# Normalising the rows of a second LayerNorm on GpSimd instead of VectorE, with five score products one unit earlier

## The reference

```python
x = x + xattn(layernorm(x), ctx, ctx, mask, Wq, bq, Wk, bk, Wv, bv, Wo, bo, 16)   # 16 heads of 16
x = x + ffn(layernorm(x), Ws1, bs1, Ws2, bs2, We1, be1, We2, be2, Wr, br)

def layernorm(x, eps=1e-5):
    m, v = mean(x, -1), var(x, -1)
    return (x - m) / sqrt(v + eps)
```

## Time and profile before

| | us |
|---|---|
| runs | 1044.37 median of 3 (1043.41 to 1051.45) |
| profiled execution | 1049.24 |
| its span | 1047.6 |
| PE busy in the span | 944.4 (90%) |
| DVE busy | 709.0 (68%) |
| ACT busy | 577.4 (55%) |
| POOL busy | 380.3 (36%) |
| slots begin (first transpose of the maxima, line 537) | 60.8, 99.1, 141.5, 184.5, 227.4, 270.4, 313.0, 357.0 |

### The profile page before, as it was taken

The page is one execution under the profiler, slowest core; times in us unless marked ns, Lnnn a source line. Parts: engine busy times, 40 slices in busy tenths (PEclk is TensorE's granted clock), DMA queues, the critical chain, the costliest instruction groups (busy, mean ns, idle before and its releaser), DMA issues.

```text
span 1047.6 us, 26860 instructions
## 1 busy us (share of the span) xinstructions
PE 944.4 (90%) x7515; PEld 691.6 (66%) x7515; DVE 709.0 (68%) x1822; ACT 577.4 (55%) x1296; POOL 380.3 (36%) x547
## 2 busy tenths in 40 slices
PE   5588999999997887979999799999799999999996
PEld 4223445545453345758778698888588888888885
DVE  5776778888787545636686666777357667667753
ACT  3126566665655564323544565677346666656653
POOL 5300131635526252142420443444323443433342
PEclk9779999999999989989999999999999999999999
DMA  4543424455253131247554553455224544535232
GB/s 153 136 103 75 107 70 120 134 135 135 73 151 94 34 141 61 62 179 240 198 190 128 155 138 54 132 134 142 41 36 129 143 92 96 137 49 141 44 53 43
DMA packets 107927, 117.34 MB, mean 112 GB/s; under 512 B 20396, under 2 KB 99960, under 8 KB 107648
## 3 DMA queue, kind: packets, MB, share of 16 engines
q1 hardware_dynamic: 87168, 67.97, 23.7%
q0 software_dynamic: 20064, 47.20, 18.1%
q10 hardware_dynamic: 560, 0.53, 0.1%
HBM read 73.91 MB, written 38.87 MB: 108 GB/s over the span
## 4 chain that ended last, share of the span: by engine, by line
PE 38%; issue 6%; DMA 5%; DVE 3%; SPq 2%; ACT 1%; ACTq 1%; DVEq 0%; another core or an unknown queue 0%; POOL 0%; POOLq 0%
PE ff_psH L2329 22%; PE ff_psY L2356 13%; DMA ff_xrow<-expert_in 2%; PE ff_psX L2283 2%; DMA ff_x<-out_dram 1%; DVE ff_actf L2582 1%; DMA ff_xrow<-xn 1%; PE ff_psH L2298 1%; DMA expert_in<-ff_zeros 1%; PE ff_psY L2313 1%; DMA out_dram<-ff_x 1%; DVE ff_actl L2575 1%; SPq L1995 0%; ACT ff_gel L2423 0%; DVE ff_ysb L2659 0%
## 5 line engine op out<-in xcount | busy, mean ns | idle before, releaser
L2329 PE MATMUL ff_psH<-xh,ff_wx 128*128 128x256 f16 (+1 forms) x1776 | 269.6, 263 | 15.4 <-issue 10.3
L2329 PE MATMUL ff_psH<-xl,ff_wx 128*128 128x256 f16 (+1 forms) x888 | 217.5, 263 | 0.0
L1136 DVE TENSOR_REDUCE fast_negm<-fast_psS 128x2 f32<-128x512 f32 x256 | 167.8, 686 | 72.9 <-PE fast_psS L515 70.4
L894 ACT ACTIVATE fast_PT<-fast_psT 128x512 f32<-128x512 f32 x256 | 147.0, 595 | 94.2 <-PE fast_psT L547 92.7
L2264 POOL DMA_INDIRECT out_dram<-ff_ysc,ff_trow x78 | 124.8, 1600 | 195.8 <-ACT ff_ysc L2471 181.5
L2329 PEld LDWEIGHTS ff_psH<-xh,ff_wx 128*128 128x128 f16 x1776 | 166.7, 99 | 37.3 <-issue 14.8
L2582 DVE SCALAR_TENSOR_TENSOR ff_actf<-ff_psH,ff_b1T,ff_gel 128x256 f32<-128x256 f32 (+1 forms) x234 | 106.1, 454 | 103.5 <-ACT ff_gel L2423 102.0
L2423 ACT ACTIVATE ff_gel<-ff_psH,ff_b1T 128x256 f32<-128x256 f32 (+1 forms) x234 | 105.4, 451 | 83.2 <-PE ff_psH L2329 64.0
L2356 PE MATMUL ff_psY<-ff_wx,ff_acth 128*128 128x256 f16 x792 | 132.4, 273 | 0.6 <-DVE ff_actl L2575 0.5
L2418 ACT ACTIVATE ff_acth<-ff_actf 128x256 f16<-128x256 f32 (+1 forms) x282 | 110.7, 393 | 34.4 <-DVE ff_actf L2582 32.8
L515 PE MATMUL fast_psS<-fast_Kz,fast_Qs 128*128 128x512 f16 x256 | 101.2, 400 | 24.8 <-DVE fast_negm L1136 16.9
(11 more groups left out here) (279 smaller groups left out, 1691.8 us busy)
## 6 DMA issues: line engine op xcount, KB each, us to landing
ff_st<-in_L_ffn_We_dram POOLq DMA_DIRECT2D x12, 1536.0 KB
ff_xrow<-expert_in SPq DMA_DIRECT2D x41, 256.0 KB
ff_st<-in_L_ffn_We_dram POOLq DMA_DIRECT2D x12, 768.0 KB
fast_Qs<-qstk SPq DMA_DIRECT2D x48, 128.0 KB
fast_xbuf<-in_x_dram SPq DMA_DIRECT2D x8, 512.0 KB, 3.9
fast_words<-in_mask_BxSxS_bk_dram SPq DMA_DIRECT2D x8, 512.0 KB
fast_xres<-in_x_dram SPq DMA_DIRECT2D x8, 512.0 KB, 4.2
out_dram<-fast_x1s SPq DMA_DIRECT2D x8, 512.0 KB, 5.4
```

The source lines that it names most:

```text
L894: nc.scalar.activation(PT[:, n % NPT, :], psT[n % 2][:], ACT.Exp).then_inc(sem["exp_done"], 1)
L1136: nc.vector.tensor_reduce(negm[:, two(b), t, 2 * p:2 * p + 2], src, AX.X, ALU.max, negate=True).then_inc(sem["max_done"], 1)
L2329: mm = nc.tensor.matmul(psH[j % stage.banks][:, (half + 1) * NB - rows:(half + 1) * NB], a[:, dt, lo:lo + P], x[:, dt, NB - rows:], start= ...
```

## The change

The four normalising instructions of the second norm go from VectorE's list to GpSimd's, right behind rstd2 of the same batch; the semaphore xn2_ready, for which TensorE and SP wait, is now raised by GpSimd. In `SCORES` unit 1 gets 5 products instead of 4 and unit 6 gets 4 instead of 5, for TensorE and VectorE alike; the running sums are 5, 10, 15, 19, 24, 28, 32 where they were 4, 9, 14, 18, 23, 28, 32. A place for a maximum in VectorE's unit 1 goes; the maximum itself is taken a line later by `rest`.

```diff
-SCORES = (0, 4, 5, 5, 4, 5, 5, 4)
+SCORES = (0, 5, 5, 5, 4, 5, 4, 4)
...
             begin(1)
             if real(b - 1):
                 normalised_out(b - 1, 1)
-            one_maximum()
-            if real(b - 2):
-                ln2(b - 2)
             rest()
...
             normalised_out(last, 1)
-            ln2(last - 1)
             early_blocks.row_low(dve, 0)
...
             low(1, 0)
-            ln2(last)
             gate(1, 2)
...
+        def ln2(b):
+            until(pool, "rstd2", of("rstd2", b, 1))
+            for t in range(QT):
+                ins = nc.gpsimd.tensor_scalar(xn2_of(b)[:, t, 0:D], xres[:, t, :], mv2[:, t, 0:1], rstd2[:, t:t + 1],
+                                              ALU.subtract, ALU.mult)
+            ins.then_inc(sem["xn2_ready"], 1)
+
...
             if real(b - 2):
                 rstd2_(b - 2)
+                ln2(b - 2)
             if real(b - 4) and not left_over(b - 4):
                 rows_out(b - 4)
```

## The result

The changed kernel takes **1061.9 us** by the median of 4 runs (1058.55 to 1064.15), the kernel before, run beside it, 1044.03 (4 runs, 1043.41 to 1051.45). The ratio on record for the runs side by side is 1.014, 95% interval 1.0116 to 1.0164: slower by some 15 us (12 to 17). The two medians by themselves lie 17.9 us apart; with four runs of each, the four of before spread over 8 us, that is the coarser measure. The forecast was 1047.9 and no change; the range ended at 1056.

A forecast was written before the change was run, and what follows sets the result against it. TensorE's own queue was taken as the bound. Slot 6, slot 7 and tail -0.3, VectorE beside GpSimd +1.5 and +0.6, products +1.7 gave +3.5 us: 1047.9 us, range 1041 to 1056.

The forecast's parts named there:

- part 2: The four normalising instructions on GpSimd: 2.8 us taken, between 0.9 and 3.7; middle slots would not wait for the rows.
- the addition: GpSimd's adding of a vector to the same xres rows, 2.78 us for four, taken as the nearest row for the duration.
- rival B: More contention: at 3.7 us on GpSimd the queue shifts 2.6, x1s also covers the comparison; +7.8 us, 1052.2, chance 0.12.
- 1.7 for the products: Cost of the moved score products on TensorE: +0.34 us in each of slots 1 to 5.
- the forecast's 1.5 for contention: Slots 3 to 5: GpSimd's shifted bias on xres slows VectorE's cast, gap and pick, 0.5 us each slot.
- Part 1: Four instructions leave VectorE: worth nothing to TensorE in slots 2 to 5, up to 1.2 us once in slot 6.
- The 1.2 us wait in slot 6: TensorE's product waiting 1.23 us for a maximum queued behind VectorE's four normalising instructions; the removal was to save it.
- Part 3: GpSimd's queue behind the four comes 1.7 us later, beside VectorE's work: 1.5 us in slots 3 to 5, 0.6 in slot 6.
- the rule on two SBUF inputs: VectorE instructions with two SBUF inputs contend with GpSimd's SBUF reads; single-input ones outside two-port modes and PSUM maxima don't.
- Part 4: Score products one unit earlier: new 0.5 us loss ending unit 1, 0.2 saved in unit 6; slot 0 nothing.
- A: Faster by 1 to 4 us: GpSimd takes about VectorE's 0.34 us an instruction, nothing shifts; -1.4 us, 1043.0, chance 0.20.
- C: Slower by over 1%: TensorE waits before the transposes in each slot from 1.6 us an instruction; about +17, 1061, chance 0.08.

The follow-up runs named there:

- The forms: Changed kernel with each of the four GpSimd instructions given its own mix of operations and scalars; executed once, 1045.66 us, time not used because it routes other rows.
- taking them back: Changed kernel with the rows of batches 4 to 7 (slots 6, 7 and tail) normalised on VectorE again; ratio 1.0081 to the kernel before.
- the kernel with halves: Changed kernel with two of the four row tiles normalised on GpSimd and two on VectorE, new SCORES kept; ratio 1.0046 to the kernel before.
- the table alone: Kernel before with only the new SCORES, the normalising left on VectorE; ratio 1.0026 to the kernel before.

## Why the prediction was wrong

**The step that failed** is the duration in part 2: "I take that: 2.8 us, between 0.9 and 3.7". It is 4.86 us for four, beyond both ends. Both were drawn through the wrong rows. The line for the upper end joined a row with 4 elements and one with 128 elements, one operation, a half-width output and no scalar of a partition; the addition has two inputs, but no second operation. The forms show that the scalar operation is the dearer kind (0.86 against 0.74) and that the second operation and the scalars add 0.37.

**The rest of the sum carries most of the loss once it has the right duration.** Fed with 4.86 us, the same steps say: the rows in slot 6 at 316.30 + 4.86 = 321.2 for 320.0, a loss of 1.2; in slot 7 at 365.15 for 362.36, 2.8; in the tail at 402.9 for 401.1, 1.8; the last batch, whose wait was 0.2 of the 3.4, has 0.89 now, 0.7 more (measured, not from a step). That is 6.4 before rounding, and taking them back gave 6 us (1.0081 for 1.014). In the profiles slot 6 alone gives back 2.9 us, where its step says 1.2: 1.1 of it is TensorE's longer busy time at the lower clock, for which the sum had no term. The queue is 3.7 us late instead of 1.7, so x1s lies over the comparison (rival B's 0.6 in each of three slots) and the bias over the routing (0.5 in each): 3.3. With 1.7 for the products this makes 11.4 of 14.9. At 2.5 us on GpSimd the kernel with halves took +4.8, and the +3.5 forecast for 2.8 lies within its interval; that is in part luck, since the forecast's 1.5 for contention wasn't there and slot 2 had 1.8 instead.

**Point by point.** Part 1: that VectorE's freed time is worth nothing in the middle slots held, and more than that: what it gained it lost again by contention. The 1.2 us wait in slot 6 was 0.21 us after, but another of 1.6 us for a maximum came later in the slot, and the waits for maxima there fell only from 2.9 to 2.5. Part 3: the contention was given the right instructions (comparison, cast, picks; the gap kept its 0.15 us in the change) and about the right size each, 0.4 to 0.6 us, but at a shift of 1.7 us, where the bias would touch the routing and x1s nothing; at 2.5 us on GpSimd slots 3 to 5 lost nothing by the bias, although one cast took 0.61 us, so the 1.5 us was too much there. Its reading of the trace for the rule on two SBUF inputs was wrong: the instruction that went from 0.26 to 0.76 us (`fast_diff<-fast_sums`, line 1240) has one tensor input, as the cast has, so these rows don't bear on the case of two inputs; the comparison's other two instructions do (0.22 to 0.75 and 0.43 to 0.85 us with the table alone, line 1242 and 1245). What the rule was used for, that the maxima stay free, was right. Part 4: +0.34 for slots 3 to 5 held exactly, term by term; for slots 1 and 2 it didn't (0 and +1.3), and slot 0, put at 0, has +0.7 with the table alone. What it left out is that between unit 1 and unit 6 all work is 0.74 us later; in slot 2 that put the comparison under the bias, 1.0 us more that no step had.

**The rivals.** A needed 0.34 us an instruction, which VectorE takes; it was 1.22. The prediction cites the Trainium skill for A (GPSIMD Engine Reference, "Engine selection": one-input work roughly at line rate); these runs don't agree, 0.86 us on GpSimd with a single operation against 0.34 on VectorE with two. C named the right quantity and the wrong threshold. It said that TensorE stands in each slot from 1.6 us an instruction on; at 1.22 it stands in slots 6 and 7 and the tail alone, and contention, which C added only as an extra, brings as much. The loss of over 1% began well below the point that the text gave for it. Its sum is wrong too: at 1.6 us four take 6.4, which shifts the queue by 6.4 - 1.1 = 5.3 us and not 4.7, and 3.5 + 3 x 3.6 + 2 + 3.6 is +20, not +17. B had the mechanism in the middle slots, and its +7.8 at 3.7 us stands well between the halves' +4.8 and the change's +14.9. That an instruction's cost may lie beyond any row deserved more than the 0.10 for slower.

**Open.** The steps leave 3.5 of the 14.9 us. Slots 1 and 2 have 1.0 of it, slot 0 has 0.7, which the table alone brings too, and the fill 1.0 and the feed-forward part 0.6 are of the size by which they scatter. Nor do the steps for a middle slot stand alone: without the products' shift the same contention cost 1.6 to 2.0 us in each of slots 3 to 5, with it the whole is 1.2 to 1.6. In slot 6 TensorE is busy 1.07 us longer than before at a clock of 0.93 (38.65 against 37.58 at 0.96), and the wait for VectorE's V is 0.8 us longer; with the table alone it is 1.0 longer, so it need not be the rows' doing. What lowers the clock there isn't known. In the tail the granted clock of 413 to 449 is 0.91, where the matching stretch of before (403 to 435) had 0.98. TensorE had just waited 5.1 us there. The wait alone doesn't set it: from 46 us behind the start of slot 7 on, the five kernels with that wait have 0.91 to 0.95, the six with a wait of 1.6 to 3.2 us have 0.94 to 0.98.

## What to carry to other kernels

Before work is moved to another engine, find a row of exactly that form on it: the number of operations and where the scalars come from, not only shape and tile. If there is none, the upper end of its cost lies beyond the nearest rows, and the sum is made at that end too. A longer instruction costs also through what is queued behind it: look at what the shifted queue will lie beside; here that was about as much as the late rows. Two operations with nothing between them that both wait for another engine belong where that engine has slack: here their place was worth 0.4% in all, and nothing in the slots where that engine sets the pace.

## What the runs showed of the hardware

A scalar operation on GpSimd over 256 fp32 elements a partition takes 0.86 us with one constant and 1.22 with two scalars of a partition, against 0.74 for an addition of two tensors; VectorE takes 0.34 for the same (1.37 for four). GpSimd's additions stretch VectorE's small instructions from SBUF that run beside them: a cast of 128 x 8 from 0.17 to 0.66 us, the two picks from 0.32 to 0.84, the comparison's first instruction from 0.26 to 0.65, the same four normalising instructions from 1.38 to 3.02. The four casts looked at end 0.02 to 0.03 us behind the GpSimd instruction under way, so each lost what was left of that one, and one that began late in it took only 0.19 us. The cast and the comparison's first instruction, which the forecast had put at risk, and the four normalising ones, which it hadn't looked at, have one tensor input each. By the section of the Trainium skill that the prediction cites (SBUF — State Buffer, "Who interferes with whom") that is no exception: it names `cast` and `tensor_scalar` among the operations that can take the shared ports when their operands meet its conditions, and these rows agree.
